# 4,096-key attention: ScalarE copies the next unit's row of negated maxima ahead of exponential 14 of a unit in place of 15

## What is computed

```python
energy = jnp.einsum('nqhd,nkhd->nhqk', q, k)
energy = jnp.where(mask == 0, jnp.float32(-1e+20), energy)
attn = jax.nn.softmax(energy / math.sqrt(EMBED), axis=3)
out = jnp.einsum('nhql,nlhd->nqhd', attn, v).reshape(N, q_len, HEADS * HEAD_DIM)
return out @ w_out.T + b_out
```

## Time and profile before

| | us |
|---|---|
| median of 3 runs (893.89, 893.99, 899.29) | 893.99 |
| profiled execution, its own time | 893.57 |
| span of the profile, first to last instruction | 891.9 |
| copies of the row, first and last start | 397.1 and 761.4 |

### The profile page before, as it was taken

The page is one execution under the profiler, slowest core; times in us unless marked ns, Lnnn a source line. Parts: engine busy times, 40 slices in busy tenths (PEclk is TensorE's granted clock), DMA queues, the critical chain, the costliest instruction groups (busy, mean ns, idle before and its releaser), DMA issues.

```text
span 891.9 us, 19675 instructions
## 1 busy us (share of the span) xinstructions
PE 858.8 (96%) x6818; PEld 524.5 (59%) x6818; DVE 595.4 (67%) x1534; ACT 491.3 (55%) x935; POOL 420.2 (47%) x394
## 2 busy tenths in 40 slices
PE   8999999999999999889999999999999999889998
PEld 7888887557567656644444444444444444567656
DVE  2476555664523222878888888888888888379875
ACT  3344443551112122678888888888888888632010
POOL 1332222000241010168888888888888888522000
PEclk9999999999999999999999999999999999999999
DMA  7944497904515613896566655566655562710220
GB/s 241 299 172 161 169 364 279 337 6 154 163 44 83 119 37 140 233 267 137 77 90 88 85 76 76 69 87 87 85 76 76 70 88 96 126 48 1 49 49 24
DMA packets 78391, 109.86 MB, mean 123 GB/s; under 512 B 27036, under 2 KB 64544, under 8 KB 74307
## 3 DMA queue, kind: packets, MB, share of 16 engines
q1 hardware_dynamic: 73019, 93.70, 48.5%
q0 software_dynamic: 4960, 14.96, 4.5%
q10 hardware_dynamic: 360, 0.50, 0.3%
HBM read 86.29 MB, written 21.06 MB: 120 GB/s over the span
## 4 chain that ended last, share of the span: by engine, by line
PE 84%; DVE 7%; SPq 3%; issue 2%; DMA 2%; ACT 2%; ACTq 0%; POOL 0%; DVEq 0%
PE bank L1538 15%; PE bank L1565 14%; PE bank L1512 7%; PE bank L1391 6%; PE bank L1194 5%; PE bank L1181 5%; PE bank L1550 4%; PE bank L1419 3%; PE bank L1800 3%; PE bank L1359 2%; PE bank L1147 2%; PE bank L1277 2%; PE bank L1268 2%; PE bank L1860 2%; SPq L500 1%
## 5 line engine op out<-in xcount | busy, mean ns | idle before, releaser
L759 POOL TENSOR_TENSOR region<-region 128x512 int32<-128x512 int32 x256 | 321.4, 1276 | 61.0 <-ACT region L1042 61.0
L1042 ACT ACTIVATE region<-bank 128x512 f32<-128x512 f32 x512 | 279.6, 596 | 59.9 <-PE bank L1550 48.0
L2287 DVE CUSTOM_DVE_ANT_0 xnT<-bank,region 128x1024 bf16<-128x1024 f32 x128 | 156.1, 1220 | 51.9 <-issue 51.4
L1538 PE MATMUL bank<-region 128*128 (+1 forms) x1024 | 158.5, 276 | 7.7 <-ACT region L1024 5.2
L2287 DVE CUSTOM_DVE_ANT_0 region<-bank,region 128x1024 bf16<-128x1024 f32 x128 | 156.1, 1220 | 0.0
L1538 PEld LDWEIGHTS bank<-region 128*128 128x128 bf16 x1024 | 79.7, 100 | 112.9 <-ACT region L1042 65.2
L1565 PE MATMUL bank<-region 128*32 128x256 f32 x2048 | 139.7, 387 | 0.0
L1565 PEld LDWEIGHTS bank<-region 128*32 128x32 f32 x2048 | 59.1, 109 | 46.9 <-issue 15.6
L706 POOL DMA_DIRECT2D keys_split<-region x48 | 35.8, 748 | 98.2 <-DVE region L2052 98.2
L1512 PE MATMUL bank<-region,xnT 64*128 64x512 bf16 x244 | 73.5, 381 | 0.0
L1514 PE MATMUL bank<-region,xnT 64*128 64x512 bf16 x244 | 73.5, 381 | 0.0
(11 more groups left out here) (395 smaller groups left out, 1324.3 us busy)
## 6 DMA issues: line engine op xcount, KB each, us to landing
region<-keys_split SPq DMA_DIRECT2D x224, 128.0 KB, 5.0
region<-in_ctx SPq DMA_DIRECT2D x32, 512.0 KB, 7.4
keys_split<-region POOLq DMA_DIRECT2D x48, 256.0 KB, 4.1
region<-in_L_ffn_we_gate SPq DMA_DIRECT2D x8, 688.0 KB
region<-in_L_ffn_we_up SPq DMA_DIRECT2D x8, 688.0 KB
region<-in_mask_1x1xSxS_ik SPq DMA_DIRECT2D x1, 4096.0 KB, 16.5
region<-in_L_ffn_we_down SPq DMA_DIRECT2D x8, 512.0 KB
mask_kept<-region SPq DMA_DIRECT2D x1, 2048.0 KB, 9.4
```

The costliest lines, as they stand in the source:

```text
L759: nc.gpsimd.tensor_tensor(out=bits, in0=bits, in1=keep4[k], op=ALU.mult).then_inc(probs_kept, 1)
L1042: nc.scalar.activation(prob4[n % PROBS].rearrange("p a b -> p (a b)"), bank[:, SCORE4[n], :], ACT.Exp, scale=SCALE4).then_inc(exp4_ready, 1)
L1538: last = mm(bank[:, SCORE4[n], k * S:(k + 1) * S], slab[s][:, t * P:(t + 1) * P], qT4[:, bass.ds(u, 1), :].rearrange("p o q -> p (o q)"), ...
L2287: v.tensor_tensor_reduce(out=junk[q], in0=bank[:, 3 + 2 * q:5 + 2 * q, :].rearrange("p a b -> p (a b)"), in1=maskN[:, q, 2 * c * CH:2 * (c ...
```

## The change

One number: in a unit with a next one, ScalarE's copy of the row moves from in front of exponential 15 to in front of exponential 14. The same instructions run, the same number of times; no other engine's program differs.

```diff
                     if n == 14 and last:
                         squares(0)
-                    if n == 15 and not last:
+                    if n == 14 and not last:
                         negmax_row(u + 1)
                     act.wait_ge(score4, HALVES * u + n + 1)
                     nc.scalar.activation(prob4[n % PROBS].rearrange("p a b -> p (a b)"), bank[:, SCORE4[n], :],
```

## The result

| | before | after |
|---|---|---|
| median over all runs beside each other (20 each) | 894.09 us | 900.22 us |
| ratio, 95% interval (914.25 and 2887.29 us of the changed kernel left out) | | 1.0061 [1.0035, 1.0086] |
| profiled execution, its own time | 893.57 | 899.39 |
| span of the profile | 891.9 | 897.7 |
| forecast | | 900.0, 897.5 to 903.0 |

A forecast was written before the change was run, and what follows sets the result against it. PE bounds the kernel, and its wait at each unit's entry adds to the period; 30 x 0.21 - 0.09 = 6.2 us on 893.57 gives 899.8, and with the median 0.4 higher 900.0 us was forecast, range 897.5 to 903.0.

The forecast's parts named there:

- What bounds the kernel; the exchange rate: Attention units: PE, busy 96% of the span, bounds; time lost at a unit's entry adds to the period one to one.
- The copy's start in the loop: ScalarE in the loop: the copy starts at 505.90, about 0.36 us after the second transpose's start.
- Exponential 14 behind the copy: ScalarE's list: exponential 14 starts 0.40 us after the copy's start, takes 0.60, done at 506.90 in place of 506.19.
- Rival 4: Behind the copy on ScalarE: exponential 14 overlaps it, an entry costs 0.08 us, 896.3 us in all; chance 0.04.
- PE's entry in the loop: PE's scores start 0.21 us later per entry, idle 0.50 in place of 0.29 us; bounds 0.16 to 0.36.
- rival 3: ScalarE's queue: exponential 14's register work runs only after the copy, 0.32 us per entry, 903.5 us; chance 0.08.
- The written-out entries: Units outside the loop: scores follow exponential 14 by 0.06 us, as they followed the copy; 0.21 us later taken.
- The entry behind copy 27: ScalarE in the loop, PE written out: the entry comes 0.21 + 0.11 = 0.32 us later.
- The sum: Over 31 copies: 4.83 + 1.05 + 0.10 + 0.32 - 0.09 = 6.2 us more.
- Nothing else moves: Exponential 15 under 0.2 us later without cost; exponential 0 and half 3 move alike; POOL, ScalarE and VectorE have spare time.
- Rivals 1 and 2: PE's entry stall: first, hidden, stays 0.29 us, 894.0 us, chance 0.06; second, all goes, 886.4 us, chance 0.02.

The follow-up runs named there:

- e1: Changed kernel, but ScalarE copies the row behind exponential 15, last in its list: 916.72 us, ratio 1.0205 to the kernel before.
- e9: Changed kernel with the loop over units 4 to 27 written out on PE and ScalarE: 897.12 us, ratio 1.0035 to the kernel before.
- e10: Changed kernel with half 0 in the row's bank, sums copied ahead of exponential 5, four-byte row copy, loop written out: 891.07 us, ratio 0.9953 to before.
- e2: Changed kernel, but half 0 uses the row's bank and half 1 that of exponential 14: 897.83 us, ratio 0.9971 to the kernel before.
- e5: Changed kernel, but PE waits for exponential 14 first and the copy second at a unit's entry: 900.06 us, ratio 1.0026 to the kernel before.
- e3: Changed kernel, but PE makes the row ahead of the mask matmuls of halves 14 and 15: 892.77 us, ratio 0.9970 to the kernel before.
- e11: Changed kernel with half 0 in the row's bank, sums copied ahead of exponential 5, four-byte row copy, loop kept: 890.72 us, ratio 0.9947 to before.
- e8: Changed kernel with the row made ahead of the masks, half 0 in the row's bank, sums ahead of exponential 5: 897.43 us, ratio 1.0004 to before.

## Why the prediction was right, and which term was mis-sized

- *What bounds the kernel; the exchange rate.* That a wait at the entry is added to the period one to one was read from two units of before. It held in e1, e9 and e10, which moved the unit by what they moved the entry, to within 0.02; in e2 the entry was won whole, but halves 1 and 6 then waited, and the unit got 0.24.
- *The copy's start in the loop.* 0.36 us after the second transpose, worked out and measured.
- *Exponential 14 behind the copy.* 0.40, worked out and measured. Rival 4, an overlap behind the copy, is out, as the rows of this very copy had said. The rule of the Trainium skill, "ScalarE: Activation LUTs", section "What ACT_TABLE_LOAD costs", that back-to-back activations overlap by about 93 ns, does not hold behind this copy: it is 0.38 us long, and the next one starts 0.40 us after its start.
- *PE's entry in the loop.* PE's idle time of 0.42 was forecast as 0.50 - 0.07 = 0.43 by the profile's count, the period of 12.39 as 12.40. The register work of exponential 14 lies under the copy, so rival 3 is out.
- *The written-out entries were the mis-sized term.* Forecast 0.21 later, measured 12.27 - 12.00 = 0.27 to 0.28 per unit. The copy and exponential 14 came when they should: 422.09 - 421.83 = 0.26 after the transpose, then 0.40. But PE's scores followed the end of exponential 14 (422.49 + 0.60 = 423.09) by 0.14, not by the 0.06 by which they had followed the end of the copy. The step that failed was to take the price of one wait for that of another. e5 shows it: with the two waits exchanged a written-out unit gets 0.08 shorter, with the same ScalarE. The entry behind copy 27, also written out on PE, was mis-sized alike: the unit before it took 12.38 in place of 11.99 (720.59 to 732.97, before 714.00 to 725.99), 0.39 where 0.32 was forecast.
- *The sum.* Six such entries at 0.07 more are 0.42 us, and the units lost 6.6 us where 6.2 was forecast. The medians lie 900.22 - 894.09 = 6.1 us apart, the profiled executions 899.39 - 893.57 = 5.8, since the rest of the program, which the change does not touch, took 0.8 us less after than before; a difference of half a us is below what whole times of this kernel tell. So that 6.1 lies so near 6.2 is luck. The recorded sum gives 893.99 + 6.2 = 900.2; the 900.0 that was forecast lies 0.2 below it.
- *Nothing else moves.* So it was: PE's busy time per turn 47.87 and 47.86, VectorE's 41.08 and 41.07, POOL's 42.21 in both.
- *Rivals 1 and 2,* hidden or won, are out: PE's stall at the entry neither stayed nor went, but grew from 0.22 to 0.42.

Left open are the 0.14 us of e3's order and why an exponential overlaps the copy of sums in front of it and not the copy of the row; no run here varied the partitions of that copy.

## What to carry to other kernels

When two results are needed by the same waiter and one engine makes them in turn, moving one ahead only decides which of them is late: a job that still waits should not stand in an in-order list ahead of one that can start. To gain from the earlier result, the need for the other has to go too (here: another bank for the first half), and each removed wait shows the next one, so the entry has to be read again after every step.

## What the runs showed of the hardware that was not expected

- Two waits for the same moment can have different prices for the waiter: in written-out code PE's scores began 0.06 us after the end of the copy and 0.14 after that of exponential 14, and there the order of the two waits in the source decides which price is paid (e5). In the loop a second register instruction behind the wait cost 0.10 us (0.52 against 0.42 in e5).
- The same bits copied as 128 four-byte numbers per row took 268 ns in place of 374 (e10), but lengthened the register instruction ahead of it from 55 to 98 ns in the loop (e11).
- Two small transposes placed between scores and mask matmuls, in place of between masks and values, made a unit about 0.2 us longer (12.10 in e8 against 11.90 in e10, neither with idle time in its turn). About 0.06 is a wait for exponential 13 that modelled ends hide. In e3 the masks start 0.20 after the first transpose (506.56 and 506.36), while in the changed kernel the values follow the second transpose by 0.06 (508.46 and 508.40).
